# Sending a mixture-of-experts layer's output rows after its last input rows, with deeper rings and one read of expert numbers for each table

## The reference

```python
x = x + tanh(g_xattn) * attention(layernorm(x), ctx, ctx, mask, Wq, bq, Wk, bk, Wv, bv, Wo, bo)   # 16 heads of 8, rotary positions
z = layernorm(x)
logits = z @ Wr + br                       # 8 experts
idx = argmax(logits); gate = softmax(logits)[idx]
y = gelu(z @ W1[idx] + b1[idx]) @ W2[idx] + b2[idx]      # 128 -> 512 -> 128, exact gelu
x = x + tanh(g_ffn) * gate * y
```

## Time and profile before

| | |
|---|---|
| median of 3 runs | 324.67 us (323.63 to 325.26) |
| the profiled execution | 324.98 us, span 323.2 us |
| PE busy (matmul) | 247.2 us, 76% |
| VectorE busy | 196.2 us, 61% |
| GpSimd busy | 182.6 us, 57% |
| ScalarE busy | 158.0 us, 49% |
| granted TensorE clock, mean | 0.928 of full speed |
| output scatters (L540) | 39, together 37.9 us of GpSimd |
| row scatters (L493) | 32, together 34.0 us of GpSimd |

### The profile page before, as it was taken

How to read it: one execution, slowest core, us unless ns; L and a number is a source line. 1 busy time by engine, 2 the same in 40 slices (tenths; PEclk the granted TensorE clock), 3 DMA queues, 4 the chain that set the end, 5 groups by cost and what they waited for, 6 DMA issues and landing times.

```text
span 323.2 us, 10769 instructions
## 1 busy us (share of the span) xinstructions
PE 247.2 (76%) x3593; PEld 204.9 (63%) x3593; DVE 196.2 (61%) x680; ACT 158.0 (49%) x481; POOL 182.6 (57%) x222
## 2 busy tenths in 40 slices
PE   1458898888898978788878537694559898998970
PEld 1246677676677756577656426593559697996960
DVE  5457787888988889877797506652723333243420
ACT  1244667677676847676766203431523343343420
POOL 6475647476577886687867750046254434353450
PEclk9999999999999999999999755967897999799996
DMA  7612646254636342515111212201232212111100
GB/s 223 187 20 37 180 107 181 61 163 123 160 88 157 101 123 44 126 40 139 35 38 39 63 54 60 52 21 62 61 95 64 77 57 61 43 53 44 33 26 0
DMA packets 58537, 26.64 MB, mean 82 GB/s; under 512 B 38608, under 2 KB 53989, under 8 KB 58484
## 3 DMA queue, kind: packets, MB, share of 16 engines
q1 hardware_dynamic: 55204, 20.15, 25.1%
q0 software_dynamic: 2272, 4.46, 4.3%
q10 hardware_dynamic: 1008, 1.34, 1.4%
HBM read 16.69 MB, written 5.51 MB: 69 GB/s over the span
## 4 chain that ended last, share of the span: by engine, by line
PE 33%; DVE 19%; POOL 19%; issue 14%; another core or an unknown queue 5%; ACT 3%; POOLq 2%; DMA 1%; SPq 0%; DVEq 0%; ACTq 0%
PE ps L728 12%; POOL rot L528 5%; POOL rot L522 5%; POOL rot_s L524 5%; PE ps L710 3%; PE ps L712 3%; PE ps L711 3%; PE ps L763 2%; DVE qk L1161 2%; POOLq L91 2%; DVE mx L1195 2%; POOL stk L507 2%; DVE stk L1212 2%; PE ps L775 2%
## 5 line engine op out<-in xcount | busy, mean ns | idle before, releaser
L540 POOL DMA_INDIRECT out<-fin,got x39 | 37.9, 972 | 50.5 <-DVE fin L1260 35.9
L1195 DVE TENSOR_REDUCE mx<-ps 128x16 f16<-128x1024 f32 x32 | 39.1, 1221 | 22.1 <-PE ps L799 11.5
L728 PE MATMUL ps<-w_f,hT 128*128 x312 | 49.0, 305 | 0.0
L1260 DVE SCALAR_TENSOR_TENSOR fin<-ps,got 128x128 f32<-128x128 f32 x39 | 13.7, 351 | 57.2 <-PE ps L728 38.6
L728 PEld LDWEIGHTS ps<-w_f,hT 128*128 128x128 f32 x312 | 42.0, 209 | 1.1 <-issue 0.2
L522 POOL TENSOR_TENSOR rot<-qk,cf 128x256 f32<-128x256 f32 x32 | 23.4, 731 | 31.0 <-ACT qk L589 22.5
L493 POOL DMA_INDIRECT rows<-x_all,dest_i x32 | 34.0, 1062 | 8.2 <-issue 5.1
L817 PE MATMUL ps<-qT,kbd 128*128 128x64 f16 x512 | 34.8, 196 | 3.8 <-issue 3.8
L638 ACT ACTIVATE hT<-ps 128x512 f32<-128x512 f32 x39 | 23.3, 598 | 29.3 <-PE ps L712 24.0
L814 PE MATMUL ps<-mxT,ch 128*128 128x128 f16 x256 | 34.7, 225 | 2.0 <-issue 2.0
L569 ACT ACTIVATE pr<-ps 128x1024 f32<-128x1024 f32 x32 | 32.8, 1024 | 4.2 <-PE ps L817 3.3
(11 more groups left out here) (160 smaller groups left out, 638.9 us busy)
## 6 DMA issues: line engine op xcount, KB each, us to landing
kbd<-kT SPq DMA_DIRECT2D x128, 32.0 KB
got<-rows SPq DMA_DIRECT2D x39, 72.0 KB
w_f<-in_W_rows SPq DMA_DIRECT2D x8, 256.0 KB, 2.9
w_r<-in_W_last_row SPq DMA_DIRECT2D x8, 256.0 KB, 3.1
w_f<-in_L_ffn_W SPq DMA_DIRECT2D x8, 256.0 KB
x_all<-in_x SPq DMA_DIRECT2D x3, 512.0 KB, 4.7
xt_all<-in_x_t SPq DMA_DIRECT2D x3, 512.0 KB, 4.4
ct_all<-in_ctx SPq DMA_DIRECT2D x3, 512.0 KB, 4.4
```

Of the source, the lines that this page charges most:

```text
L540: pool.indirect_dma_start(out=out_d, out_offset=bass.IndirectOffsetOnAxis(ap=got_i[:, u % GOT, R_ID:R_ID + 1], axis=0), in_=fin[:, u % FRI ...
L728: mm = pe.matmul(o, hT[:, par, c, :], w2_f[:, bass.ds(e, 1), c, :].rearrange("p o n -> p (o n)"), start=False, stop=(c == FC - 1))
L1195: dve.tensor_reduce(mx[:, t % 2, 0:H], ps_s[:, :].rearrange("p (h k) -> p h k", k=S), AX.X, ALU.max).then_inc(mx_done, 1)
```

## The change

Three things change.

- **Order on GpSimd.** An output scatter may only be sent in a step after the last row scatter's (step 42), and from step 43 on two in a step until they have caught up. By `out_step`, outputs 0 and 1 go in step 43, 2 and 3 in step 44, and so on up to 8 and 9 in step 47. From tile 10 on an output goes in the step in which it went before. GpSimd no longer waits for a result ahead of a row scatter.
- **Rings.** `GOT` goes from 12 to 20 and `FRING` from 8 to 20. There is one semaphore for two neighbouring buffers (`pair`), so a wait for a tile is one for its pair as far as it goes by then. Tile 14 is the last of a pair, so that no pair belongs to both tables. A fetch waits for the output 20 tiles back, a result for the one 20 tiles back.
- **Expert numbers.** PE reads all 15 numbers of the first table ahead of tile 0, and all 24 of the second ahead of tile 15. SyncE still reads its offsets eight at a time.

```diff
-GOT = 12
+GOT = 20
...
-FRING = 8
+FRING = 20
...
-        f_got = [sem(f"ffn_loaded{i}") for i in range(GOT)]
-        f_st = [sem(f"ffn_scattered{i}") for i in range(FRING)]
+        f_got = [sem(f"ffn_pair_loaded{i}") for i in range(GOT // 2)]
+        f_st = [sem(f"ffn_pair_scattered{i}") for i in range(FRING // 2)]
...
+        def pair(u):
+            return (u + N1 % 2) // 2
+
+        def pair_count(u, ring):
+
+            return 16 * sum(1 for v in range(NS) if pair(v) % ring == pair(u) % ring and pair(v) <= pair(u))
+
+        def out_step(u):
+            return max(F0 + 3 + u, max(SCATTER_AT) + 1 + u // 2)
...
-                    sp.wait_ge(f_st[u % FRING], 16 * (u // FRING + 1))
+                    sp.wait_ge(f_st[pair(u) % (FRING // 2)], pair_count(u, FRING // 2))
                     alone(sp, sp_passed)
-                sp.dma_start(got[:, slot, :], rows[bass.ds(offset, P), :]).then_inc(f_got[slot], 16)
+                sp.dma_start(got[:, slot, :], rows[bass.ds(offset, P), :]).then_inc(f_got[pair(t) % (GOT // 2)], 16)
...
-                u = i - F0 - 3
-                if tile(u):
+                for u in range(NS):
+                    if out_step(u) != i:
+                        continue
                     pool.wait_ge(f_fin, u + 1)
                     alone(pool, pool_passed)
                     pool.indirect_dma_start(
...
-                        bounds_check=B * S - 1, oob_is_err=False).then_inc(f_st[u % FRING], 16)
+                        bounds_check=B * S - 1, oob_is_err=False).then_inc(f_st[pair(u) % (FRING // 2)], 16)
 
             pipeline(step)
-            for s in range(FRING):
-                pool.wait_ge(f_st[s], 16 * len(range(s, NS, FRING)))
+            for s in range(FRING // 2):
+                pool.wait_ge(f_st[s], 16 * sum(1 for u in range(NS) if pair(u) % (FRING // 2) == s))
...
-                a, b = (0, N1) if u < N1 else (N1, NS)
-                if (u - a) % 8 == 0:
+                if u in (0, N1):
+                    a, b = (0, N1) if u < N1 else (N1, NS)
                     pe.wait_ge(g_te, 1 if u < N1 else 2)
-                    n = min(8, b - u)
                     regs = nc.values_load_multi_w_load_instructions(
-                        te_i[0:1, u:u + n], engines=[PE_ENGINE], min_val=0, max_val=NE - 1,
+                        te_i[0:1, a:b], engines=[PE_ENGINE], min_val=0, max_val=NE - 1,
...
-                    experts.update({u + m: r for m, r in enumerate(regs)})
+                    experts.update({a + m: r for m, r in enumerate(regs)})
...
-                    dve.wait_ge(f_got[s], 16 * (u // GOT + 1))
+                    dve.wait_ge(f_got[pair(u) % (GOT // 2)], pair_count(u, GOT // 2))
...
-                    wait(dve, f_st[s], 16 * (u // FRING))
+                    if u >= FRING:
+                        v = u - FRING
+                        dve.wait_ge(f_st[pair(v) % (FRING // 2)], pair_count(v, FRING // 2))
```

## The result

The changed kernel took 327.25 us (median of five runs, 326.63 to 327.82), the kernel before 325.26 us beside it (five runs, 323.63 to 325.7). The ratio is 1.0064, 95% interval 1.0034 to 1.0094: slower by 2 us (0.6%), where no change (324.6 us) was forecast. Its profiled execution took 326.63 us, span 324.8 us, against 324.98 and 323.2 before.

The account below looks back on a forecast made before the run. It took PE's steady run, delayed by unbroken indirect DMA runs on GpSimd, to bound the kernel. Scatters +0.6 and reads -0.7 gave -0.1 us: 324.9 us profiled, 324.6 us as median, range 320.0 to 327.8.

Parts of the forecast that it names:

- the sum of the reads, -0.7 us: PE's reads of expert numbers: 0.8 + 3.1 + 0.9 - 3.4 - 2.1 = -0.7 us, bounds -5.5 and +2.5.
- the stop at the second read, +3.1 and +0.9: Ahead of tile 15: a 5.2 us read of 24 numbers adds 3.1 us, the lower clock after the stop 0.9.
- the gaps at tiles 23 and 31, -5.5: Reads at tiles 23 and 31 go: -3.4 us from tile 22 to 25, -2.1 us from tile 30 to 32.
- What bounds the kernel: Unbroken indirect DMA runs on GpSimd hold PE's results; the start of PE's steady run after 245 us sets the time.
- The first run: GpSimd's DMAs from 214.75 us: six instead of eight, ending 2.55 us earlier at 222.16; last row scatters from 228.4.
- The second run, the term +0.6 us: Nine DMAs, 228.4 to 239.9 us, hold PE from 231.5 to 241.3; total held time 17.5 us against 16.8, taken as +0.6.
- The rival of the catch-up run: Nine DMAs in a row stop PE, tile 4's result caught inside; +2.4 and 0.3 for the clock: 327.3 us, chance 0.22.
- The rings, zero: Rings of 20 and pair waits on fetches and results: counted as nothing; 2 us at the first tiles if cover were gone.
- The first read, +0.8 us: PE's read before tile 0: 15 numbers in six accesses, 1.6 us instead of 0.785, with nothing hiding it.
- The rival that reads the first list singly: The 15 numbers before tile 0 are read one by one, 3.4 us: +1.8 us, 326.4 us, chance 0.10.
- the cheap reads: Rival: long reads stay near 0.8 and 2.1 to 2.6 us; reads worth -5.0 us: 320.3 us, chance 0.18.
- The rival "only row scatters hold PE": Output scatters on GpSimd are harmless to PE; scatters give -5.0, reads -0.7 us: 319.3 us, chance 0.10.

Follow-up runs that it names:

- e13: The kernel before with only the two long reads of expert numbers (15 and 24), on a chip with holds: 325.94 us, 1.0026.
- e7: The kernel before, each indirect DMA of GpSimd waiting until the previous one has landed: 391.72 us, 1.2024.
- e14: The kernel before, at most two indirect DMAs in flight from the 14th row scatter to output 4, on a chip with holds: 318.41 us, 0.979.
- e12: The changed kernel with expert numbers read by eights again (new order and rings only), on a chip with holds: 325.8 us, 1.0020.
- e3: The kernel before with only the new rings and pair semaphores, old order and reads, on a chip without holds: 305.35 us, 1.0004.
- e8: The kernel before with only the two long reads (15 and 24), on a chip without holds: 305.21 us, 0.9997.
- e11: The kernel before with reads of 15 and 24, the second list from word 16, on a chip without holds: 300.59 us, 0.9825.
- e6: The changed kernel again, without an edit, on another chip with holds: 327.13 us, 1.0059 against the kernel before.
- e17: The changed kernel with the second list stored from word 16, on a chip with holds: 322.39 us, 0.9897 against the kernel before.
- e15: The kernel before with reads of 15 and 24, second list from word 16, two DMAs in flight up to output 11, chip with holds: 314.8 us, 0.9649.

## Why the prediction was wrong, point by point

- **The step that failed: the sum of the reads, -0.7 us.** The traces show +0.6 and e13 measured +1.1 (by its interval, 0.1 to 1.6). Two terms of it were mis-sized: the stop at the second read, +3.1 and +0.9, which was +5.16, and the gaps at tiles 23 and 31, -5.5, which were -4.93. The points on the reads below take them one by one.
- **What bounds the kernel: right.** Runs of indirect DMAs hold what PE completes (e7 needs 11 us less from tile 0 to 9, and in e14 tile 9 comes 13 us earlier), and the steady run behind them sets the end. What I did not know is that this is so on some chips only.
- **The first run: right.** It ends at 223.4 (by the prediction 222.16; the whole run came 1.2 us later, behind the longer first read), tile 2's result is at 224.81 (224.9), the gates at 228.01 (228.1), the last rows from 229.11 (228.4).
- **The second run, the term +0.6 us: near in size, wrong in its course.** The two pairs of profiles have +0.74 and +0.81 us between tiles 0 and 14, and e12 measured +0.95 us (by its interval, 0 to 1.3) for the order with its rings. "Held until 1.4 us after the end, 241.3" became 242.1: the run started 0.7 us later and the hold outlasted it by 1.9 us. PE passed nothing in the second half of it. The second layer behind the release runs at the lower clock level (1.2 GHz; eight matmuls in 2.07 us, 1.15 before; granted clock 0.66 and not 0.85 over 225 to 250 us). Tile 9 is transposed at 244.93, where I had named 242 to 243.5. The count of DMAs was off by one: before, the two runs have eight and six, 14 with the one at 232.74, and not 14 and that one; after, they have 15.
- **The rival of the catch-up run: in part.** PE did stop in the second half of the run. But tile 4's result was not caught inside, VectorE had it at 232.69, and PE began two tiles, not less than one, between 231.5 and 241.3. Its price of 2.4 us was too high: of the 2.74 us at tile 9, 1.33 were there at tile 0, so tiles 0 to 9 cost +1.4 us, and 0.7 came back by tile 14. That its 327.3 us is nearly the measured 327.25 is luck: a good half of the 2 us came from the reads or from before tile 0, and not from this run.
- **The rings, zero: borne out where there are no holds** (e3: 1.0004). Under holds they were not tried alone.
- **The first read, +0.8 us: right in mechanism,** 1.77 us and so +0.98. The rival that reads the first list singly falls with it (it needed 3.4 us), and so do the cheap reads with the second.
- **The second read and what follows, +3.1 and +0.9 us: mis-sized.** The path was right and the cost too low. The read took 5.91 us and not 5.2. That is (5.91 - 0.39) / 24 = 0.23 us a number, where 0.2 had been fitted. PE stood still for 5.32 us instead of 4.6, the clock granted in 262 to 268 us was 0.55, and tiles 14 to 17 cost +5.16 us in place of +4.0. Of that, 0.63 came back between tiles 17 and 22, which the prediction did not have. My upper bound for a number, 0.26, had covered this.
- **The reads at tiles 23 and 31, -5.5 us: mis-sized too, -4.93** (tiles 22 to 32 took 19.96 us). The prediction counted each gap against a pace of 1.99 us and looked at no tile behind it. But before, tiles 25 to 30 take 9.43 us, 0.5 less than five steps of 1.99: the old stop was already giving back part of its cost, and that went with it.
- **The sum.** For the reads the measured terms give 0.98 + 5.16 - 0.63 - 4.93 = +0.58 us; I had -0.7. With +0.74 for the order and the 0.35 us that the profile before was ahead at tile 0 already, it is the +1.67 us at tile 32. By the ratios it is +1.1 (e13) and +0.95 (e12), with intervals of some 0.7 us to each side. Either way the errors on the two parts have the same sign. Two rivals' times were also added up wrongly: 324.6 + 0.6 - 5.0 is 320.2 and not 320.3, and 324.6 - 5.0 - 0.7 is 318.9 and not 319.3, which moves nothing here.
- **The rival "only row scatters hold PE" falls:** in e14 eight outputs without a row scatter between them bring back a wait of 7.01 us.

## What to carry to other kernels

A queue that has been relieved early sends what it owes in one run later: look at where the runs of indirect DMAs fall and what PE can pass under each, and not at their number alone. When lists are read into registers, see where each starts before making them longer: from word 16 and not 15 was worth 4.6 us here (e8 to e11), and turns this change from 1.006 to 0.990 (e6, e17). When a stop is taken out, look at the tiles behind it too: it may already have given something back. Compare a small effect on more than one chip, with the unchanged kernel beside it: here each part cost 0.2 to 0.3% on one kind of chip and nothing that could be measured on the other.

## What was not expected of the hardware

- The unchanged kernel takes 305.4 us on two chips and 325 us on three. Of the 20 us, 18 are there at tile 9, behind the holds, at the same pace of DMAs, 1.275 us. Why some chips have them was not found: the trace shows the wait, called remote, and not what it waits for.
- The holds shrink with two indirect DMAs in flight (0.979 on a chip with holds, 1.0119 on one without) and are absent with one. What exactly sets one off stays open (e14, e15): number in flight and distance were not varied apart, and three in flight was not tried.
- A register load costs by where its list starts: 24 numbers in 1.65 us from word 16 and 5.91 us from word 15 (0.07 and 0.25 us a number), the same on both kinds of chip. The Trainium skill ("Runtime: NRT & Kernel Launch", Instruction fetch mechanics) puts a register load at about 200 ns per register, in bulk too: the trace agrees roughly from word 15 and not from word 16.
- Behind a stop PE passes some tiles at 1.78 us in place of 1.99, after two or three slow ones at the lower clock (tiles 17 to 22 in 9.34 us, against 9.97 before), so that a stop gives back some 0.6 us. The granted clock is 1.00 in both (280.59 to 285.94 and 265 to 271 us of the kernel before), so it is not the clock. No run here shows why.
